# End states' squares folded from 64 to 16 columns a batch by two additions on GpSimd, one product of 64 columns with the means, VectorE sums 64

## Chip, cores and metric

One Trainium2 chip, one of its cores. The metric is device time in microseconds (us), from the first to the last instruction of one execution; lower is better. Engines are named as the profile names them: PE is TensorE (PEld its weight load), DVE is VectorE, ACT is ScalarE, POOL is GpSimd, SP is SyncE.

## What is computed

A state-space block with a residual and a layer norm, then a mixture of experts (8 experts, top 2, capacity 768) with a second residual and layer norm, all float32. The inputs are 8 sequences of 1024 steps of 256 features. The part in question is the recurrence over time, for each sequence, over 512 channels with 16 states each:

```python
def step(h, inp):
    dA_t, dB_t, x_t, C_t, t = inp
    h = h * dA_t + dB_t * x_t[:, :, None]
    nrm = jnp.sqrt(jnp.sum(h * h, axis=(1, 2), keepdims=True))
    fac = jnp.minimum(20.0 / (nrm + 1e-08), 1.0)
    h = jnp.where(t % 10 == 0, h * fac, h)
    y = jnp.einsum('bdn,bn->bd', h, C_t) + D_param * x_t
    return (h, y)
```

At every tenth step the whole state of a sequence (512 x 16 numbers) is scaled by a factor that comes from its norm.

## The kernel before

The recurrence is cut into tiles of T = 20 steps (NB = 52 tiles, index i), each tile into two chunks of 10 steps, and each chunk into two groups of four sequences. A chunk of one group is a batch q (NQ = 208, four batches in a tile; q = 4i + r, and r = 0 to 3 is the batch's place in its tile). Channels lie on the 128 partitions, four blocks a of them. Every engine runs the same loop, `for i in range(-4, NB + 3): for s in range(16)`, where slot s = 4r + u stands for sequence u of batch r. What an engine does in a slot is written by hand, in program order, and semaphores join the engines. There is no scheduler.

In slot u of batch q VectorE writes the products dB*x to PSUM (`mult`, L579), copies in the scaled end states that came out of batch q-2 (`carry`, L596, from tile CAR), and runs the recurrence of sequence u as one scan over 704 columns (`scan`, L610, into H). GpSimd multiplies H by C (L775, into H, one for each u), and TensorE sums these products over the 16 states with the identity (`y_sum`, L816 and L820). Between these stand the pieces of other tiles: projections, convolution, step sizes (ScalarE's L514 and L377 make the decays DA), output projection and norm. `dt_x` on VectorE (L566, twice a tile, in slots 2 and 6, just behind `norm_sum`) multiplies DT and XC, which both lie in SBUF, into PSUM.

The norms go round four engines. After the last scan of batch q-1:

1. ScalarE squares the end states, 4 sequences x 64 columns, into SQ (L398), first in slot u = 0 of batch q.
2. TensorE multiplies SQ by MEAN, a 128 x 128 matrix of 1/256, which sums over the partitions: two products of 4 x 32 = 128 columns (L862), accumulated in `NP`, in slot u = 0 of batch q.
3. VectorE sums `NP` to one number for each sequence (`norm_sum`, L617, tile SN), in slot u = 2, between `mult` and the scan.
4. GpSimd, in slot u = 2 ahead of its product L775: power -0.5 (L755), factor (L757), and end states times factor into CAR (L760).
5. VectorE's `carry` in slot u = 0 of batch q+1 waits for CAR:

```python
if u == 0:
    eng.wait_ge(s_car, q - 1)
eng.tensor_copy(o, CAR[:, u:u + 2]).then_inc(s_ca, 1)
```

GpSimd's other work in a tile: L750 in slot 1, the layer norm's L780, L781, L783 and L786 in slot 3, L793 and L797 in slot 7, L726 in slot 8, L730 in slot 10, L737 and L743 in slot 14.

Of the kernel before, what the change touches and what calls it, by code (L numbers as in the profile page):

```python
# [8 lines left out]
ALU = mybir.AluOpType  # L9
# [9 lines left out]
NQ = 2 * NC  # L19
# [82 lines left out]
def ssm_phase(nc, d, YA, X2d, LGd, Bd, Cd, RB, IOE):  # L102
    ctx = ExitStack()
    with ctx:
        def sb(name, shape, dt=F32):
            return ctx.enter_context(nc.sbuf_tensor(name, shape, dt))

        def sem(name):
            return ctx.enter_context(nc.semaphore(name))
# [11 lines left out]
        MEAN = sb("MEAN", [128, 128])  # L121
# [29 lines left out]
        SQ = sb("SQ", [128, 4, 64])  # L151
# [9 lines left out]
        YB = [ctx.enter_context(nc.psum_tensor(f"YB{i}", [128, 512], F32)) for i in range(2)]  # L161
# [12 lines left out]
        s_bcs, s_ln, s_dth, s_tg, s_z64, s_da, s_x2t, s_hsq = (  # L174
            sem("bcs"), sem("sp"), sem("dth"), sem("tg"), sem("z64"), sem("da"), sem("x2t"), sem("hsq"))

        s_halo, s_sgh, s_dx, s_dxh, s_hc, s_slot = sem("halo"), sem("sgh"), sem("dx"), sem("dxh"), sem("hc"), sem("slot")
        s_min, s_dt, s_xn, s_pow, s_fac, s_car = (
            sem("min"), sem("dt"), sem("xn"), sem("pow"), sem("fac"), sem("car"))
        s_ve, s_sd, s_x2 = sem("ve"), sem("sd"), sem("x2")  # L180
# [2 lines left out]
        s_nrm, s_ys, s_op, s_tr, s_lg = sem("nrm"), sem("ys"), sem("op"), sem("tr"), sem("lg")  # L183
# [22 lines left out]
        def cols(c):  # L206
            return 11 if c < NC - 1 else 1 + (L - 1) % 10


        def rows(c):  # L210
            return min(10, cols(c))
# [12 lines left out]
            return YB[q % 2][:, 0:160]  # L224

        def NP(q):
            return YB[1 - q % 2][:, 256:384]


        def two(j):  # L230
# [2 lines left out]
        def one(j):  # L233
            return 16 * (j // 2 + 1)
# [292 lines left out]
        def vector_program(eng):  # L527
# [85 lines left out]
            def norm_sum(q):  # L613
                eng.wait_ge(s_nrm, q + 1)
                if q >= 2:
                    eng.wait_ge(s_pow, q - 1)
                eng.tensor_reduce(SN[:, q % 2], NP(q).rearrange("p (u a) -> p u a", u=4), AX.X,  # L617
                                  ALU.add).then_inc(s_red, 1)
# [97 lines left out]
        def gpsimd_program(eng):  # L716
            eng.wait_ge(s_pre, PRE_CV)
            for i in range(-4, NB + 3):
                live = ok(i)
                for s in range(16):  # L720
                    r, u = s // 4, s % 4
                    q = 4 * i + r
# [28 lines left out]
                    if u == 2 and 1 <= q <= NQ - 2:  # L751

                        p = q - 1
# [9 lines left out]
                    if i == NB - 2 and s == 0:  # L763

                        k = cols(NC - 1)
                        eng.memset(DA[:, (NC - 1) % 4].rearrange("p b a n t -> p b (a n t)")[:, :, 0:64 * k].rearrange(
                            "p b (a t) -> p b a t", t=k)[:, :, :, 0], 0.0).then_inc(s_slot, 1)
                    if live:
                        k, n = cols(q // 2), rows(q // 2)
                        h = H[:, q % 3, u, 0:64 * k].rearrange("p (a n t) -> p a n t", a=4, n=16)[:, :, :, 0:n]  # L770
                        cb = CB[:, q % 2, :, u, 0:n].unsqueeze(1).to_broadcast([128, 4, 16, n])
                        if u == 0:
                            eng.wait_ge(s_cb[q % 2], one(q))
                        eng.wait_ge(s_scan, 4 * q + u + 1)
                        eng.tensor_tensor(h, h, cb, ALU.mult).then_inc(s_hc, 1)  # L775
# [23 lines left out]
        def tensor_program(eng):  # L799
            def y_sum(q, n0, n1):  # L800
                if not 0 <= q < NQ:
                    return
                k, w = cols(q // 2), rows(q // 2)
                hv = H[:, q % 3, :, 0:64 * k].rearrange("p u (a n t) -> p u a n t", a=4, n=16)
                yv = YP(q).rearrange("p (u a t) -> p u a t", u=4, a=4)[:, :, :, 0:w]
                if n0 == 0:
                    c, g = q // 2, q % 2
                    j, cc = c // 2, c % 2
                    eng.wait_ge(s_dx, j + 1)
                    if j > 0:  # L810
                        eng.wait_ge(s_dxh, j)
                    if q >= 2:
                        eng.wait_ge(s_z, q - 1)
                    if 1 <= q < NQ:
                        eng.wait_ge(s_red, min(q, NQ - 2))
                    eng.matmul(yv, ID[:], DX[:, j % 2, :, 4 * g:4 * g + 4, 10 * cc:10 * cc + w].rearrange(  # L816
                        "p a b t -> p b a t"), start=True, stop=False)
                    eng.wait_ge(s_hc, 4 * (q + 1))
                for n in range(n0, n1):
                    mm = eng.matmul(yv, ID[:], hv[:, :, :, n, 0:w], start=False, stop=n == 15)  # L820
                mm.then_inc(s_ys, 1)
# [28 lines left out]
            for i in range(-4, NB + 3):  # L850
                if i == 0:
                    eng.wait_ge(s_pre, N_PRE)
                for s in range(16):
                    r, u = s // 4, s % 4
                    q = 4 * i + r
                    if u == 0:
                        y_sum(q - 2, 11, 16)
                    if u == 0 and 1 <= q <= NQ - 2:
                        p = q - 1
                        eng.wait_ge(s_hsq, q)  # L860
                        for a in range(2):
                            mm = eng.matmul(NP(p), MEAN[:], SQ[:, :, 32 * a:32 * a + 32], start=a == 0, stop=a == 1)  # L862
                        mm.then_inc(s_nrm, 1)
                    if u == 2:
                        y_sum(q - 1, 0, 6)
                    if u == 3:
# [1 line left out]
                    if s == 0 and ok(i + 3):  # L868
# [3 lines left out]
                        for a in range(2):  # L872
                            mm = eng.matmul(PA[:, 320:480], MEAN[:], TB[:, a].rearrange("p b t -> p (b t)"),
                                            start=a == 0, stop=a == 1)
# [23 lines left out]
                    if s == 7 and ok(i + 2):  # L898
                        j = i + 2
                        dt_proj(j, 0, PZ)  # L900
                        for k in range(4):
                            mm = eng.matmul(PZ[0:64, 320:480], WBC[:, k, :],
                                            XC[:, j % 2, k].rearrange("p b t -> p (b t)"), start=k == 0, stop=k == 3)
                        mm.then_inc(s_dtp, 1)
                    if s == 9 and ok(i - 2):
# [3 lines left out]
                        for g in range(2):  # L909
                            for a in range(2):  # L910
                                mm = eng.transpose(PA[:, 80 * (2 * g + a):80 * (2 * g + a) + 80],
                                                   VV[:, g, 128 * a:128 * a + 128], ID[0:80, 0:80])
                        mm.then_inc(s_tr, 1)
                    if s == 10 and ok(i - 1):
# [4 lines left out]
                        for g in range(2):  # L919
                            for a in range(4):  # L920
                                mm = eng.matmul(PZ[0:80, 256 * g:256 * g + 256], zf[:, a, 80 * g:80 * g + 80],  # L921
                                                WO[:, a, :], start=a == 0, stop=a == 3)
                        mm.then_inc(s_op, 1)
                    if s == 12 and ok(i - 2):
# [3 lines left out]
                        for g in range(2):  # L928
                            for a in range(2):
                                mm = eng.matmul(PA[0:80, 320 + 8 * g:328 + 8 * g], X2T[:, 2 * g + a, :], WR[:, a, :],  # L930
                                                start=a == 0, stop=a == 1)
# [11 lines left out]
        with nc.Block() as block:  # L943
            @block.sync
            def _(eng):
                sync_program(eng)

            @block.scalar
            def _(eng):
                scalar_program(eng)  # L950

            @block.vector
            def _(eng):
                vector_program(eng)

            @block.gpsimd
            def _(eng):
                gpsimd_program(eng)

            @block.tensor  # L960
            def _(eng):
                tensor_program(eng)
# [423 lines left out]
def build(nc, d, out):  # L1386
    YA = nc.dram_tensor("YA", [B * LP, DM], F32, kind="Internal").ap()
    X2d = nc.dram_tensor("X2d", [B * LP, DM], F32, kind="Internal").ap()
    LGd = nc.dram_tensor("LGd", [128, 8 * B, E], F32, kind="Internal").ap()
    Bd = nc.dram_tensor("Bd", [NC, 2, NS, 40], F32, kind="Internal").ap()  # L1390
    Cd = nc.dram_tensor("Cd", [NC, 2, NS, 40], F32, kind="Internal").ap()
    with ExitStack() as ctx:
        RB = ctx.enter_context(nc.sbuf_tensor("RB", [128, 4096], F32))
        IOE = ctx.enter_context(nc.sbuf_tensor("IOE", [128, 8], F32))
        ssm_phase(nc, d, YA, X2d, LGd, Bd, Cd, RB[:], IOE[:])
        moe_phase(nc, d, YA, X2d, LGd, out, RB[:])
# [43 lines left out]
```

## Time and profile before

| what | us |
|---|---|
| median of 3 runs | 2777.07 |
| lowest and highest run | 2772.13, 2777.97 |
| profiled execution, span from first to last instruction | 2772.7 |
| busy in it: PE, DVE, ACT, POOL | 2593.0, 2382.4, 2245.1, 2134.4 |
| granted TensorE clock, mean over the span | 0.975 |

The profile gives the profiled execution's own time as its span; nothing lies around it. The recurrence takes the span from about 100 to 2280 us, and the experts take the rest. A tile of the recurrence takes 42.9 us: GpSimd's L775 of r = 0, slot 0 starts at 1191.37 in one tile and at 1234.26 in the next.

### The profile page before, as it was taken

To read this page: it belongs to the slowest core of one execution; us is meant where nothing else is said; L and a number is where in the kernel's file an instruction comes from. 1 tells how busy PE (TensorE), PEld (TensorE's weight loads), DVE (VectorE), ACT (ScalarE), POOL (GpSimd) and SP (SyncE) were. 2 spreads that over 40 slices of the span, in tenths; PEclk is the share of its full clock that TensorE was granted. 3 is DMA by queue.
4 is the path that set the end of the run, shared out by engine and by line. 5 is a ranking of instruction groups with operands and counts; after the bars stand their busy time and mean duration, and the time that the engine had idled before them with its cause. 6 is when DMAs were issued, how large, how long until landed. Compare 5 with 4: busy or idle time off the path is not lost. (4 is left out here: it accounts for less than half of the span.)

```text
span 2772.7 us, 50775 instructions
## 1 busy us (share of the span) xinstructions
PE 2593.0 (94%) x16812; PEld 2388.8 (86%) x16812; DVE 2382.4 (86%) x3391; ACT 2245.1 (81%) x5074; POOL 2134.4 (77%) x2237
## 2 busy tenths in 40 slices
PE   5899999999999999999999999999999986899992
PEld 4899999999999999999999999999999975677762
DVE  2999999999999999999999999999999997221124
ACT  5999999999999999999999999999999962111113
POOL 0789888898898988989889889898898883434314
PEclk9899999999999999999999999999999987999996
DMA  1222222222222222222222222222222222234227
GB/s 61 70 78 78 79 80 78 78 78 81 77 78 75 80 79 78 78 78 82 78 78 78 81 78 78 76 78 80 78 78 78 75 78 93 48 93 105 61 48 254
DMA packets 145746, 225.65 MB, mean 81 GB/s; under 512 B 37836, under 2 KB 84684, under 8 KB 144332
## 3 DMA queue, kind: packets, MB, share of 16 engines
q1 hardware_dynamic: 123044, 188.95, 22.4%
q0 software_dynamic: 9216, 12.59, 2.6%
q10 hardware_dynamic: 13224, 20.86, 2.2%
q8 instruction: 134, 2.20, 0.3%
q14 instruction: 128, 1.05, 0.1%
HBM read 189.27 MB, written 33.05 MB: 80 GB/s over the span
## 5 line engine op out<-in xcount | busy, mean ns | idle before, releaser
L775 POOL TENSOR_TENSOR H<-H,CB 128x640 f32<-128x640 f32 (+1 forms) x832 | 1216.2, 1476 | 157.1 <-DVE H L610 154.9
L610 DVE TENSOR_TENSOR_SCAN H<-DA,PM 128x704 f32<-128x704 f32 (+1 forms) x832 | 1309.4, 1594 | 0.0
L514 ACT ACTIVATE DA<-DT,SM 128x160 f32<-128x160 f32 (+1 forms) x3328 | 1106.8, 421 | 1.6 <-POOL DT L737 0.3
L820 PE MATMUL YB<-H,ID 128*128 128x160 f32 (+1 forms) x6656 | 1043.9, 309 | 0.2 <-POOL H L775 0.2
L820 PEld LDWEIGHTS YB<-H,ID 128*128 128x128 f32 x6656 | 982.3, 191 | 16.4 <-issue 11.2
L579 DVE TENSOR_TENSOR PM<-PM,BB 128x640 f32<-128x640 f32 (+1 forms) x832 | 673.1, 809 | 0.0
L377 ACT ACTIVATE DA<-DA 128x2560 f32<-128x2560 f32 (+1 forms) x206 | 477.7, 2319 | 1.7
L755 POOL TENSOR_TENSOR FC<-SN,HALF 128x4 f32<-128x4 f32 x206 | 232.8, 1130 | 40.8 <-DVE SN L617 36.8
L826 PE MATMUL PAZ<-XN,RB 128*128 128x160 f32 x1664 | 254.7, 307 | 0.1
L836 PEld LDWEIGHTS PAZ<-XB,CD 128*128 128x128 f32 x1664 | 237.5, 188 | 16.8
L845 PE MATMUL PAZ<-XC,RB 128*128 128x160 f32 x1664 | 244.4, 300 | 3.3 <-DVE XC L647 3.3
L1285 POOL DMA_INDIRECT YA<-YS,IG x48 | 75.1, 1566 | 219.8 <-ACT YS L1116 208.2
L836 PE MATMUL PAZ<-XB,CD 128*128 128x160 f32 x1664 | 243.1, 297 | 0.0
L826 PEld LDWEIGHTS PAZ<-XN,RB 128*128 128x128 f32 x1664 | 237.9, 195 | 0.7 <-ACT CS L467 0.3
L845 PEld LDWEIGHTS PAZ<-XC,RB 128*128 128x128 f32 x1664 | 231.1, 190 | 6.4 <-DVE XC L647 4.0
L921 PE MATMUL PAZ<-WO,Z 128*80 128x256 f32 x832 | 189.1, 380 | 0.0
L862 PE MATMUL YB<-SQ,MEAN 128*128 128x128 f32 x824 | 131.3, 282 | 43.0 <-ACT SQ L398 43.0
L760 POOL TENSOR_TENSOR CAR<-H,FC 128x256 f32<-128x256 f32 x206 | 155.4, 754 | 17.3
L921 PEld LDWEIGHTS PAZ<-WO,Z 128*80 128x80 f32 x832 | 125.3, 151 | 49.4 <-issue 0.7
L1359 PE MATMUL PE<-W,HT 128*128 128x256 f32 x768 | 167.2, 379 | 0.8 <-issue 0.8
L1348 PE MATMUL PE<-XTE,W 128*128 128x384 f32 x512 | 167.3, 488 | 0.0
L1359 PEld LDWEIGHTS PE<-W,HT 128*128 128x128 f32 x768 | 145.3, 190 | 20.8 <-issue 1.3
(157 smaller groups left out, 2779.7 us busy)
## 6 DMA issues: line engine op xcount, KB each, us to landing
BB<-Bd SPq DMA_DIRECT2D x208, 320.0 KB, 3.4
CB<-Cd SPq DMA_DIRECT2D x208, 320.0 KB, 3.2
W<-in_w ACTq DMA_DIRECT2D x16, 1024.0 KB, 7.9
XT<-in_xT SPq DMA_DIRECT2D x52, 160.0 KB, 2.2
XR<-in_xp SPq DMA_DIRECT2D x208, 40.0 KB
X2d<-VV SPq DMA_DIRECT2D x208, 40.0 KB
YA<-VV SPq DMA_DIRECT2D x208, 40.0 KB
HI<-YA SPq DMA_DIRECT2D x6, 1024.0 KB, 9.9
```

Source lines behind the costliest of these rows:

```text
L377: eng.activation(v, v, ACT.Exp, scale=16.0).then_inc(s_da, 1)
L514: eng.activation(DA[:, c0 + k0:c0 + k1, :, a, m, 1:11].rearrange("p c b t -> p b c t"), DT[:, j % 2, a].rearrange("p b (c t) -> p b c t", ...
L579: eng.tensor_tensor(DBX(u)[:, 0:64 * k].rearrange("p (a n t) -> p a n t", a=4, n=16)[:, :, :, 1:k], U(c)[:, :, 4 * g + u, 0:k - 1].unsquee ...
L610: eng.tensor_tensor_scan(H[:, q % 3, u, 0:n], decays(c, g)[:, u], DBX(u)[:, 0:n], 0.0, ALU.mult, ALU.add).then_inc(s_scan, 1)
L755: eng.tensor_tensor(FC[:, p % 2], SN[:, p % 2], HALF[:], ALU.pow).then_inc(s_pow, 1)
L775: eng.tensor_tensor(h, h, cb, ALU.mult).then_inc(s_hc, 1)
L820: mm = eng.matmul(yv, ID[:], hv[:, :, :, n, 0:w], start=False, stop=n == 15)
L826: mm = eng.matmul(p[:, 160 * a:160 * a + 160], WIN[:, k, c0 + 128 * a:c0 + 128 * a + 128], XN[:, j % 2, k], start=k == 0, stop=k == 1)
L836: mm = eng.matmul(p[:, 160 * a:160 * a + 160].rearrange("p (b t) -> p b t", b=8), CD[:, k, 2 * m + a], XB[:, 2 * m + a, :, k:k + 20], star ...
L845: mm = eng.matmul(p[:, 160 * a:160 * a + 160], WDT[:, k, c:c + 128], XC[:, j % 2, k].rearrange("p b t -> p (b t)"), start=k == 0, stop=k == 3)
L921: mm = eng.matmul(PZ[0:80, 256 * g:256 * g + 256], zf[:, a, 80 * g:80 * g + 80], WO[:, a, :], start=a == 0, stop=a == 3)
L1359: t = eng.matmul(bank(n)[:, 256 * h:256 * h + 256], HT[:, m, 128 * (2 * c + h):128 * (2 * c + h) + 128], W2[:, e % 2, m, :], start=m == 0, ...
```

## The change

The squares are folded on GpSimd before they go to TensorE. At the start of slot u = 0 of every batch, ahead of its product L775, GpSimd waits for SQ, adds columns 32 to 63 of each sequence to columns 0 to 31, waits for that, and adds columns 16 to 31 to 0 to 15. TensorE then does one product of 4 x 16 = 64 columns where it did two of 128, and does it in slot u = 1 in place of u = 0. VectorE sums 64 numbers to 4 where it summed 128 to 4. The result is the same up to the order of additions.

```diff
@@
+        s_half, s_fold = sem("half"), sem("fold")
@@
         def NP(q):
-            return YB[1 - q % 2][:, 256:384]
+            return YB[1 - q % 2][:, 256:320]
@@ gpsimd_program
+                    if u == 0 and 1 <= q <= NQ - 2:
+
+                        eng.wait_ge(s_hsq, q)
+                        eng.tensor_tensor(SQ[:, :, 0:32], SQ[:, :, 0:32], SQ[:, :, 32:64], ALU.add).then_inc(s_half, 1)
+                        eng.wait_ge(s_half, q)
+                        eng.tensor_tensor(SQ[:, :, 0:16], SQ[:, :, 0:16], SQ[:, :, 16:32], ALU.add).then_inc(s_fold, 1)
                     if live:
@@ tensor_program
-                    if u == 0 and 1 <= q <= NQ - 2:
+                    if u == 1 and 1 <= q <= NQ - 2:
                         p = q - 1
-                        eng.wait_ge(s_hsq, q)
-                        for a in range(2):
-                            mm = eng.matmul(NP(p), MEAN[:], SQ[:, :, 32 * a:32 * a + 32], start=a == 0, stop=a == 1)
-                        mm.then_inc(s_nrm, 1)
+                        eng.wait_ge(s_fold, p + 1)
+                        eng.matmul(NP(p), MEAN[:], SQ[:, :, 0:16], start=True, stop=True).then_inc(s_nrm, 1)
```

On GpSimd this is the stretch from slot 7 to slot 10 of a tile (r = 1 to r = 2), before the change, with the semaphores that each instruction waits for:

```order
L793 TENSOR_TENSOR DX<-XC,SM 128x32x20 [waits xc,ys]
L797 COPY DX<-DX 128x32
L726 COPY XB<-XB 128x32x3 [waits cv]
L775 TENSOR_TENSOR H<-H,CB 128x64x10 [waits scan,cb0]
L775 TENSOR_TENSOR H<-H,CB 128x64x10 [waits scan]
L730 TENSOR_SCALAR TA<-TA 128x640 [waits ex]
L755 TENSOR_TENSOR FC<-SN,HALF 128x4 [waits red]
L757 TENSOR_SCALAR FC<-FC 128x4 [waits pow]
L760 TENSOR_TENSOR CAR<-H,FC 128x256 [waits ca,fac]
```

And with the change (its lines are numbered anew: L782 is L775, L756 is L755, and so on):

```order
L800 TENSOR_TENSOR DX<-XC,SM 128x32x20 [waits xc,ys]
L804 COPY DX<-DX 128x32
L727 COPY XB<-XB 128x32x3 [waits cv]
L772 TENSOR_TENSOR SQ<-SQ 128x4x32 [waits hsq]
L774 TENSOR_TENSOR SQ<-SQ 128x4x16 [waits half]
L782 TENSOR_TENSOR H<-H,CB 128x64x10 [waits scan,cb0]
L782 TENSOR_TENSOR H<-H,CB 128x64x10 [waits scan]
L731 TENSOR_SCALAR TA<-TA 128x640 [waits ex]
L756 TENSOR_TENSOR FC<-SN,HALF 128x4 [waits red]
L758 TENSOR_SCALAR FC<-FC 128x4 [waits pow]
L761 TENSOR_TENSOR CAR<-H,FC 128x256 [waits ca,fac]
```

The two additions stand ahead of four long instructions and of the three that make CAR. The same pair stands in this place in the other three batches of a tile.

On TensorE this is the stretch around the product with the means in the tile's batch r = 1, before the change:

```order
L820 MATMUL YB1<-H,ID 128x160 x5
L862 MATMUL YB1<-SQ,MEAN 128x128 x2
L816 MATMUL YB0<-DX,ID 128x160
L820 MATMUL YB0<-H,ID 128x160 x6
L845 MATMUL PAZ<-XC,RB 128x160 x8
```

And with the change:

```order
L827 MATMUL YB1<-H,ID 128x160 x5
L868 MATMUL YB1<-SQ,MEAN 128x64
L823 MATMUL YB0<-DX,ID 128x160
L827 MATMUL YB0<-H,ID 128x160 x6
L852 MATMUL PAZ<-XC,RB 128x160 x8
```

In this batch the product keeps its neighbours, since slot 4 and slot 5 hold nothing else. In r = 0 it moves behind the eight projections of slot 0, in r = 3 behind the four products of L930 and the first four of the gate's projections.

## Rows read from the trace of the kernel before

**Rows 1.** The page's head: the span, and each engine's busy time, share and instructions.

```profile
span 2772.7 us, 50775 instructions
PE 2593.0 (94%) x16812; PEld 2388.8 (86%) x16812; DVE 2382.4 (86%) x3391; ACT 2245.1 (81%) x5074; POOL 2134.4 (77%) x2237
```

**Rows 2.** Busy time by stretch: stretch, length, engines in order, clock, DMA share, GB/s.

```profile
core 0: us, PE busy (x) PEld busy (x) DVE busy (x) ACT busy (x) POOL busy (x), PEclk, DMA share, GB/s
1000.00:1400.00 400.00, 393.46 (x2724) 373.77 (x2724) 400.00 (x544) 384.12 (x859) 354.45 (x373) 1.00 0.27 78
```

**Rows 3.** Waits in 200 to 2200 us: waiter, releaser, total, times, longest.

```profile
POOL H L775 <- DVE H L610: 132.5, 138, 2.0
PE YB L862 <- ACT SQ L398: 34.2, 47, 0.7
POOL FC L755 <- DVE SN L617: 26.7, 94, 0.4
```

**Rows 4.** Timeline of POOL over one tile: start, duration (x2: both together), [idle before].

```profile
1194.88 1.22 POOL L755 TENSOR_TENSOR FC<-SN,HALF 128x4 f32<-128x4 f32 x1 [0.34 <-DVE SN L617]
...
1202.66 2.92 POOL L775 TENSOR_TENSOR H<-H,CB 128x640 f32<-128x640 f32 x2
...
1205.80 1.25 POOL L755 TENSOR_TENSOR FC<-SN,HALF 128x4 f32<-128x4 f32 x1 [0.22 <-DVE SN L617]
...
1212.67 3.00 POOL L775 TENSOR_TENSOR H<-H,CB 128x640 f32<-128x640 f32 x2
...
1216.56 1.03 POOL L755 TENSOR_TENSOR FC<-SN,HALF 128x4 f32<-128x4 f32 x1
...
1218.00 0.75 POOL L760 TENSOR_TENSOR CAR<-H,FC 128x256 f32<-128x256 f32 x1
1218.70 2.91 POOL L775 TENSOR_TENSOR H<-H,CB 128x640 f32<-128x640 f32 x2
1222.29 1.47 POOL L775 TENSOR_TENSOR H<-H,CB 128x640 f32<-128x640 f32 x1 [0.68 <-DVE H L610]
...
1229.32 2.92 POOL L775 TENSOR_TENSOR H<-H,CB 128x640 f32<-128x640 f32 x2
1234.26 1.48 POOL L775 TENSOR_TENSOR H<-H,CB 128x640 f32<-128x640 f32 x1 [2.01 <-DVE H L610]
```

**Rows 5.** Timeline of DVE in the same tile.

```profile
1205.44 0.28 DVE L617 TENSOR_REDUCE SN<-YB 128x4 f32<-128x128 f32 x1
1205.66 0.50 DVE L566 TENSOR_TENSOR PM<-DT,XC 128x320 f32<-128x320 f32 x1
...
1219.62 0.28 DVE L596 COPY PM<-CAR 128x128 f32<-128x128 f32 x1
...
1230.78 0.16 DVE L714 COPY LGS<-PAZ 80x16 f32<-80x16 f32 x1
```

**Rows 6.** Groups of POOL by shape, whole span: count, busy us, mean ns, idle before.

```profile
L760 POOL TENSOR_TENSOR CAR<-H,FC 128x256 f32<-128x256 f32 x206 | 155.4, 754 | 17.3
L743 POOL TENSOR_TENSOR XN<-XT,RST 128x320 f32<-128x320 f32 x52 | 45.0, 865 | 20.9 <-ACT RST L493 14.0 <-PE PAZ L826 3.6
L775 POOL TENSOR_TENSOR H<-H,CB 128x256 f32<-128x256 f32 x8 | 5.7, 734 | 3.0 <-DVE H L610 2.9
L1298 POOL TENSOR_TENSOR NM<-NM,SD 128x8 f32<-128x8 f32 x8 | 1.6, 202 | 0.6
```

**Rows 7.** Timeline of POOL and DVE in one later batch; DVE L566 by itself (ns min/median/max).

```profile
2232.02 2.91 POOL L775 TENSOR_TENSOR H<-H,CB 128x640 f32<-128x640 f32 x2
2234.89 1.25 POOL L755 TENSOR_TENSOR FC<-SN,HALF 128x4 f32<-128x4 f32 x1
...
2234.31 0.97 DVE L566 TENSOR_TENSOR PM<-DT,XC 128x320 f32<-128x320 f32 x1
...
L566 DVE TENSOR_TENSOR PM<-DT,XC x104: 480/494/974, 54.0 to 2266.7; 128x320 f32<-128x320 f32 x104
```

**Rows 8.** Timeline of PE at the product with the means, r = 1 and r = 0.

```profile
1202.22 0.61 PE L862 MATMUL YB<-SQ,MEAN 128*128 128x128 f32 x4
1202.66 0.45 PE L816 MATMUL YB<-DX,ID 128*128 128x160 f32 x2
...
1231.52 0.71 PE L862 MATMUL YB<-SQ,MEAN 128*128 128x128 f32 x4 [0.72 <-ACT SQ L398]
```

## The prediction

> **What bounds the kernel now.** I read the head of the page first: PE is busiest over the whole span [rows 1], but the experts' stage has other limits, so the shares of the span don't decide. The stretches come next. In 400 us of the recurrence DVE is busy for 400.00, PE for 393.46, ACT for 384.12 and POOL for 354.45 [rows 2]. So VectorE sets the pace of the recurrence. The waits agree: POOL waits for DVE's scans and sums, TensorE waits for the squares once a tile, and DVE is nowhere among the waiters [rows 3]. PE runs so close behind that its load has to be watched, but taking work off it gives nothing by itself.
>
> POOL has 354.45 of 400 us filled, which leaves 4.9 us a tile of 42.9, and part of that is the hand-over between dependent instructions. What matters is where it lies. In one tile [rows 4] it waits 0.34 before the power of r = 0, 0.22 before that of r = 1, 0.68 before the first product of r = 3, and 2.01 before the first product of r = 0. Between the power of r = 1 (1205.80) and 1222.29 it is packed. The first two waits occur 94 times in 2000 us and sum to 26.7, which is two a tile in 47 tiles and 0.57 a tile, as in this tile [rows 3]. CAR of r = 2 is finished at 1218.75, and DVE's copy that needs it starts at 1219.62 [rows 4, 5]: 0.87 us of slack.
>
> **The change, part by part.**
>
> *VectorE's sum.* 128 columns take 0.28, and an instruction of 16 columns from PSUM takes 0.16 [rows 5]. That is 1.07 ns a column, so 64 fewer save 0.07 us. On the full engine this is gain: four a tile, 0.28 us a tile. Without any wait, 52 tiles would give 14.5 us.
>
> *TensorE.* The two products are four instructions in 0.61 us with the tail, and the next group starts 0.44 after the first [rows 8]. Half as many, of half the columns, take at most half, so about 0.25 a batch is saved, 1 us a tile; the wait of 0.72 before the squares of r = 0 goes too. PE isn't the pace, so this counts as nothing in the sum. It pays for the new wait: in r = 1 the product was ready to start at 1202.22, and the fold will be done only at about 1203.4, since POOL starts it at 1202.6. PE loses about 1.1 us there and regains it by r = 0 of the next tile. What DVE needs from the product in that batch is its sum at 1205.44, so 1.5 us of cover are left.
>
> *The fold itself, f.* The trace has no such addition. Two-input instructions of POOL take 0.202 us for 8 columns, 0.734 and 0.754 for 256, and 0.865 for 320 [rows 6]. From 8 to 320 that is 2.12 ns a column. So 128 columns come to 0.457 and 64 to 0.321. The second waits for the first: POOL's instructions that wait for another's result start 0.08 after its end (1205.44 + 0.28 = 1205.72 to 1205.80) [rows 4, 5]. Packed ones overlap by 0.03. I take **f = 0.84 us**. The bounds: below, two of the 8-column kind and the hand-over, 0.45; above, two of the 256-column kind, 1.5. Rows of 256 columns and over lie close on one line with the row of 8, so I expect 0.70 to 1.0.
>
> *Where it goes.* I carry lateness against the tile before along POOL. DVE's first sum of the tile is 0.07 early, so POOL arrives at the fold of r = 1 0.07 early. The two products that started at 1202.66 and took 2.92 now end at 1202.66 - 0.07 + f + 2.92 = 1206.35.
>
> DVE's L566 wants to start at 1205.66 - 0.14 = 1205.52, in the middle of the second product. This is the first place where it matters. In the whole trace L566 takes 494 ns in the median and once 974: at 2234.31, when POOL's second L775 was still running until 2234.93. It ended at 2235.28, 0.35 after POOL's instruction [rows 7]. It is the only two-input instruction of the loop with both inputs in SBUF on DVE. So with the fold L566 ends at 1206.35 + 0.35 = 1206.70 where it ended at 1206.16: **DVE is 0.54 late, in every tile.** The power behind it starts 0.5 late, and takes 1.25 as in that row.
>
> One delayed row is thin evidence. The Trainium skill (SBUF — State Buffer, Who interferes with whom) says that VectorE with two SBUF inputs contends with a GpSimd instruction that reads SBUF, and that whoever starts first keeps the port for its whole instruction. By this the row is the rule and the delay recurs; the power's 1.25 beside L566 and 1.03 elsewhere [rows 4] fits it. Were the row a chance, the sum would be that of the second rival below.
>
> POOL is then 0.51 late through the products of r = 1 and L793, L797, L726. The second fold, before 1212.67, makes it 0.51 + 0.84 = 1.35. CAR of r = 2 is done at 1218.75 + 1.35 = 1220.10, and with the hand-over of 0.08 DVE can copy it at 1220.18. DVE itself would be there at 1219.62 + 0.54 - 0.07 = 1220.09. So the copy starts 0.56 late, and CAR now decides, just. What is queued behind the copy on DVE is the product and the four scans of r = 3, and everything else of the loop.
>
> *Recovery.* The fold of r = 3 starts at 1218.70 + 2.91 + 1.35, about 1222.96, and ends at 1223.8: the wait of 0.68 is gone, and POOL is 1.5 late at the first product. In r = 0 it has 2.01 of idle: the products end at 1229.32 + 2.92 + about 1.25 = 1233.5, the fold at 1234.3, and the product waits anyway for DVE's scan, now at 1234.26 + 0.5. So each tile starts anew, and nothing piles up.
>
> *Sum.* DVE is 0.56 late at the copy, gains 0.07 at the sum of r = 3, and ends **0.49 us a tile late**. As a formula: with the port wait f - 0.44, with CAR 2f - 1.19, whichever is more. The layer norm's work that packs POOL in slot 3 runs from tile 2 on, so 50 tiles have both places: 50 x 0.49 = 24.5 us. The profiled span becomes 2772.7 + 24.5 = 2797.2. Its span is 4.4 below the median of the runs, so the median goes from 2777.07 to 2801.6; I say **2801**.
>
> **Rivals.** A change under 0.2% (5.5 us) counts as none, which is about what a measurement of this kernel can tell from no change.
>
> *The fold is hidden and VectorE's shorter sums show: faster.* For: DVE is full, so 0.28 us a tile is real. The place is the second product of r = 1. This rival needs it to be out of L566's way and CAR in time. From the formulas it decides at f = 0.44 with the port wait; without that wait (next rival) there is no loss below f = 0.70 and the full gain below 0.56. f would have to be like two instructions of 8 columns, against rows of 256 that take over 0.7. Full gain: 2777 - 14 = 2763. Chance 8%.
>
> *L566 does not wait in each tile.* Then the power of r = 1 starts past it and takes 1.03, not 1.25. POOL is 0.29 late at the power's end and 0.29 + 0.84 = 1.13 at CAR of r = 2: 1219.96 with the hand-over, 0.34 late, less 0.07 is 0.27 a tile, 13 us: 2790. Against: the row of 974 ns. Chance 15%.
>
> *Near zero.* The same with f of 0.70: 2 x 0.14 less, so about nothing, 2777. Chance 8%.
>
> *It does not recover in r = 0, or TensorE becomes the pace.* POOL's idle in the listed waits is 3.25 a tile, and four folds take 3.36. If f is 1.0, the formula gives 0.81 a tile, and the last fold ends at about 1235.2, past DVE's scan, so that the sum of r = 0 begins to be late too: 0.9 to 1.2 a tile, 2822 to 2837. TensorE's 1.1 us at r = 1 could add to it if its 6.5 idle us in 400 do not cover them: they do in the account above, as 1 us a tile is saved. Chance 10%.
>
> The forecast, f between 0.70 and 1.0 with the port wait, has the other 59%: 0.26 to 0.81 a tile, 2790 to 2818.
>
> **Numbers.** The range of 2783 to 2820 takes in the forecast's own and most of the second rival; it leaves out the gain, no change, and the piling up. Slower by over 0.2%: 59 + 15 + 10 = 84%. No change is the near-zero case, 8%, and faster is the first rival, 8%.
>
> **What the trace of the changed kernel would show.** The additions: two a batch, near 0.46 and 0.32 us, 206 each. The sum L617: 0.21 us. L566: half of its 104 at about 1.0 us, half at 0.49. CAR's copy in r = 3: idle of DVE just before it, or none if the port wait alone decides. POOL: no wait before its first product of r = 3, about 0.5 to 1 left in r = 0. A new wait of TensorE for the fold, about 1 us, once a tile. The tile: 43.4 us in place of 42.9. I would be wrong if the additions were much shorter than their columns say, or if L566 ran beside POOL's product at its usual length.

## The result: 0.8% slower, and the profile after

| | before | changed |
|---|---|---|
| median of 5 runs, us | 2776.85 | 2797.32 |
| lowest and highest | 2771.82, 2777.97 | 2796.19, 2798.49 |
| span of the profiled execution | 2772.7 | 2795.3 |
| one tile of the recurrence | 42.89 | 43.32 |

The ratio is 1.0081 (95% interval 1.0068 to 1.0093), which is 20.5 us slower by the medians and 22.6 by the spans. "One tile" is the time from GpSimd's copy of SG (L750, L751 after) in one tile to that in the next, the median over 49 or 50 tiles of a trace. It differs by 0.03 us or less between nearly all tiles, so it tells apart what the runs' scatter of 3 to 6 us does not. In the traces every tile from the second on loses the 0.43: the copies of SG from the second to the last are 21.5 us further apart, the first tile is 2.1 us shorter than before, and 0.4 come ahead of the first copy. The other 2.7 of the 22.6 lie behind the last copy, where the change does nothing; that part takes 508 to 513 us over the traces of this study. So the loss that the change makes is in the recurrence, in every tile, and the rest is scatter or not explained.

The page's head of the changed kernel, which answers to [rows 1]:

```profile
span 2795.3 us, 50363 instructions
PE 2555.7 (91%) x16400; PEld 2343.1 (84%) x16400; DVE 2402.9 (86%) x3391; ACT 2256.9 (81%) x5074; POOL 2278.6 (82%) x2649
```

The stretch that answers to [rows 2]:

```profile
1000.00:1400.00 400.00, 383.16 (x2629) 362.44 (x2628) 399.90 (x535) 383.11 (x861) 377.06 (x444) 1.00 0.26 77
```

POOL went from 354.45 to 377.06 busy us of 400, and PE from 393.46 to 383.16. DVE is still "busy" for 399.90, and that is the trap of this profile: it does the same work at a slower pace, because one of its instructions has become longer. The groups of DVE and POOL show which. First DVE between 200 and 2200 us, by shape:

```profile
L567 DVE TENSOR_TENSOR PM<-DT,XC 128x320 f32<-128x320 f32 x92 | 71.9, 782 | 0.5
...
L618 DVE TENSOR_REDUCE SN<-YB 128x4 f32<-128x64 f32 x185 | 37.7, 204 | 0.0
```

And POOL over the whole span:

```profile
L772 POOL TENSOR_TENSOR SQ<-SQ 128x128 f32<-128x128 f32 x206 | 94.3, 458 | 2.9 <-ACT SQ L399 2.9
...
L774 POOL TENSOR_TENSOR SQ<-SQ 128x64 f32<-128x64 f32 x206 | 66.2, 321 | 16.2
```

L567 (L566 before) had a median of 494 ns [rows 7] and now has a mean of 782: it alternates between 0.49 us in r = 0 and 1.07 in r = 1. The waits between 200 and 2200 us, against [rows 3]:

```profile
PE PAZ L878 <- ACT TB L409: 50.0, 46, 1.1
...
PE YB L868 <- POOL SQ L774: 36.5, 47, 0.9
...
POOL H L782 <- DVE H L611: 25.6, 47, 0.9
POOL FC L756 <- DVE SN L618: 12.6, 46, 0.3
```

POOL's wait for scans fell from 132.5 to 25.6, and its wait for the sum stands once in a tile now, where it stood twice. DVE has no such wait (one of 0.3 us in all): while L567 is held up it counts as busy. One tile on POOL (answers to [rows 4]):

```profile
1200.36 1.47 POOL L782 TENSOR_TENSOR H<-H,CB 128x640 f32<-128x640 f32 x1 [0.52 <-DVE H L611]
...
1211.56 0.45 POOL L772 TENSOR_TENSOR SQ<-SQ 128x128 f32<-128x128 f32 x1
1212.09 0.32 POOL L774 TENSOR_TENSOR SQ<-SQ 128x64 f32<-128x64 f32 x1
1212.37 2.92 POOL L782 TENSOR_TENSOR H<-H,CB 128x640 f32<-128x640 f32 x2
1215.24 1.30 POOL L756 TENSOR_TENSOR FC<-SN,HALF 128x4 f32<-128x4 f32 x1
...
1228.25 0.75 POOL L761 TENSOR_TENSOR CAR<-H,FC 128x256 f32<-128x256 f32 x1
```

And on DVE (answers to [rows 5]):

```profile
1203.51 0.21 DVE L618 TENSOR_REDUCE SN<-YB 128x4 f32<-128x64 f32 x1
1203.64 0.49 DVE L567 TENSOR_TENSOR PM<-DT,XC 128x320 f32<-128x320 f32 x1
...
1214.36 0.22 DVE L618 TENSOR_REDUCE SN<-YB 128x4 f32<-128x64 f32 x1
1214.59 1.07 DVE L567 TENSOR_TENSOR PM<-DT,XC 128x320 f32<-128x320 f32 x1
...
1228.33 0.80 DVE L580 TENSOR_TENSOR PM<-PM,BB 128x640 f32<-128x640 f32 x1
1229.10 0.29 DVE L597 COPY PM<-CAR 128x128 f32<-128x128 f32 x1
```

The reader is to lay these two fences over each other. POOL's second product of r = 1 ends at 1212.37 + 2.92 = 1215.29. DVE's L567 stands in its queue from 1214.59, and ends at 1215.66, 0.37 after POOL's product. It is the same in each of 40 tiles: L567 starts 2.2 behind the start of GpSimd's two products and ends 0.35 to 0.37 behind their end. In r = 0 POOL's products are over in time and the same instruction takes 0.49. Later, CAR is done at 1229.00 and the copy starts at 1229.10; packed, it would start 0.71 to 0.72 behind the product of 1228.33, at 1229.05. That is 0.05 of wait, in every tile.

### The profile page after: what moved, and what is told of

Its sections match the earlier page's. It is cut to its first block and busy times, and to the rows that moved or that the text cites. A ratio compares the mean times of both kernels' runs of the same rounds, so it can differ in the third digit from the quotient of the medians.

```text
span 2795.3 us, 50363 instructions
## 1 busy us (share of the span) xinstructions
PE 2555.7 (91%) x16400; PEld 2343.1 (84%) x16400; DVE 2402.9 (86%) x3391; ACT 2256.9 (81%) x5074; POOL 2278.6 (82%) x2649
## 3 DMA queue, kind: packets, MB, share of 16 engines
q14 instruction: 131, 1.07, 0.1%
## 5 line engine op out<-in xcount | busy, mean ns | idle before, releaser
L782 POOL TENSOR_TENSOR H<-H,CB 128x640 f32<-128x640 f32 (+1 forms) x832 | 1211.6, 1475 | 38.2 <-DVE H L611 37.8
L833 PE MATMUL PAZ<-XN,RB 128*128 128x160 f32 x1664 | 264.4, 308 | 0.4 <-DVE VV L698 0.2
L756 POOL TENSOR_TENSOR FC<-SN,HALF 128x4 f32<-128x4 f32 x206 | 234.8, 1140 | 21.5 <-DVE SN L618 17.5
L1121 ACT ACTIVATE YS<-YS,GT 128x256 f32<-128x256 f32 x48 | 21.8, 500 | 172.9 <-DVE YS L1230 172.9
```

Of the source, the lines that this page charges most:

```text
L833: mm = eng.matmul(p[:, 160 * a:160 * a + 160], WIN[:, k, c0 + 128 * a:c0 + 128 * a + 128], XN[:, j % 2, k], start=k == 0, stop=k == 1)
```

## Experiments

Times are compared with runs of the kernel before on the same chip, whose medians were 2775.5, 2773.8 and 2775.6 us in the three groups (e1 to e4, e5 to e8, e9 to e12).

### Which fold costs: e1, e2, e6, e11

The fold is done only in the batches r of a set, the others keep the old two products and the sum of 128 (the edit in part; TensorE's side and the size of the sum follow the same set):

```diff
+        FOLD = [0, 1, 3]        # e1; [0, 2, 3] in e2, [0, 3] in e6, [1] in e11
-                    if u == 0 and 1 <= q <= NQ - 2:
+                    if u == 0 and 1 <= q <= NQ - 2 and q % 4 in FOLD:
                         eng.wait_ge(s_hsq, q)
```

**e1, no fold in r = 2.**

> The changed kernel without the fold in the tile's batch r = 2 (there the old two products of 128 columns and the sum of 128). Theory (port wait): L567 (L572 here) of r = 1 still finds GpSimd's second product running, since the fold of r = 1 stands: it takes about 1.07 us in that batch, VectorE is 0.51 late behind it, and gets 0.07 back in r = 3: 0.44 us a tile, 22 us, 2799, the same as the changed kernel within 3 us, with no wait for CAR. Rival (only the late CAR of r = 2 costs): GpSimd is in time for r = 2's CAR, three shorter sums show, 0.21 a tile: 2767.

Measured: 2796.85 (2795.24 to 2797.78), ratio 1.0078 (1.0061 to 1.0095), tile 43.34. L567's counterpart takes about 1.08 in r = 1. It is the changed kernel's time with a quarter of GpSimd's new work gone. So the late CAR of r = 2 is not what costs, but for a few hundredths of a microsecond (e10).

**e2, no fold in r = 1.**

> The changed kernel without the fold in r = 1, with it in r = 0, 2 and 3. Theory: GpSimd is in time at L567 of r = 1, which takes 0.49 in all batches; the fold of r = 2 uses up the 0.87 of slack of CAR (late by at most 0.09), three shorter sums gain 0.21: 0.12 to 0.21 us a tile faster than before, 2767 to 2771. Rival (GpSimd's load decides, wherever the fold stands): three quarters of the loss stay, 2792.

Measured: 2771.22 (2770.04 to 2771.70), ratio 0.9986 (0.9976 to 0.9996), tile 42.74. The product of DT and XC takes 0.49 and 0.50 in all batches. Three folds of four cost next to nothing, and the kernel is about 0.15% faster than before, less than the 0.2% that the prediction counts as a change. That refutes the rival by which GpSimd's load decides, wherever the fold stands.

**e6, folds in r = 0 and r = 3.**

> The changed kernel with the fold only in r = 0 and r = 3, the two batches in which GpSimd waited before the change (2.01 and 0.68 us); r = 1 and r = 2 have the old products and sums. Theory: both folds fit the waits, two shorter sums gain 0.14 us a tile: tile 42.75, 2769 to 2770. Rival (three folds are better because more sums are shorter): 2.8 us slower than the kernel without the fold in r = 1 alone; or, if CAR of r = 2 was late there, the same or faster than it.

Measured: 2766.70 (2765.47 to 2768.20), ratio 0.9974 (0.9963 to 0.9985), tile 42.75. The tile agrees with the 42.75 expected. It is also that of e2 within 0.01 us: the third shorter sum of e2 gains about 0.06, and CAR of r = 2 takes 0.05 back. The 4.5 us between the medians of e2 and e6 are for the most part not in the tiles: of the 3.1 us between their traces 1.1 are there and 1.9 behind the last tile. Their groups differ by 1.8 us in the kernel before, and the rest stays unexplained.

**e11, the fold in r = 1 alone.**

> The fold in r = 1 alone, everything else as before the change. Theory: this one fold holds the whole loss and none of the gain, since VectorE's product behind the sum of r = 1 waits for another instruction anyway: VectorE 0.58 late a tile, tile 43.47, 2806. Rival (the loss needs all four folds): a quarter of it or nothing, 2772 to 2782.

Measured: 2805.17 (2803.32 to 2805.65), ratio 1.0110 (1.0094 to 1.0125), tile 43.48. One fold of four costs 0.59 us a tile, more than all four together. This is the plainest evidence in the set: its place makes the loss, and the other three only soften it.

### Is it the port: e3

VectorE's product in slot 6 takes PSUM numbers in the place of DT (the factor is left out for every other chunk):

```diff
-                eng.tensor_tensor(U(c), DT[:, j % 2, :, :, t], XC[:, j % 2, :, :, t], ALU.mult).then_inc(s_u, 1)
+                dt = DT[:, j % 2, :, :, t]
+                if c % 2 == 0 and c > 0:
+                    eng.wait_ge(s_m1, 8 * c - 9)
+                    dt = DBX(0)[:, 0:320].rearrange("p (a b t) -> p a b t", a=4, b=8)
+                eng.tensor_tensor(U(c), dt, XC[:, j % 2, :, :, t], ALU.mult).then_inc(s_u, 1)
```

> The changed kernel, but VectorE's product of DT and XC in slot 6 (the one behind the sum of r = 1) takes PSUM numbers in DT's place, so it leaves that factor out for every other chunk: one input in SBUF, all sizes, folds and waits else as changed. Theory (port wait): it takes about 0.5 us in place of 1.07 although GpSimd's product still runs; the power behind it takes 1.03; what is left is CAR of r = 2, late by 0.28 less 0.07: 0.21 us a tile, 2788. Rival (the instruction is long for another reason than its SBUF inputs): 1.07 and 2797 as in the changed kernel.

Measured: 2784.26 (2783.62 to 2785.96), ratio 1.0035 (1.0022 to 1.0048), tile 43.08. The two kinds of the product by themselves (ns min/median/max), between 200 and 2200 us DVE's copy of CAR with its idle time, and the place in one tile, POOL and then DVE:

```profile
L571 DVE TENSOR_TENSOR PM<-DT,XC x53: 480/486/646, 53.8 to 2273.0; 128x320 f32<-128x320 f32 x53
L571 DVE TENSOR_TENSOR PM<-PM,XC x51: 498/500/500, 89.5 to 2240.8; 128x320 f32<-128x320 f32 x51
```

```profile
L601 DVE COPY PM<-CAR 128x128 f32<-128x128 f32 x372 | 105.0, 282 | 10.2 <-POOL CAR L765 10.1
```

```profile
1205.52 2.93 POOL L786 TENSOR_TENSOR H<-H,CB 128x640 f32<-128x640 f32 x2
...
1207.81 0.50 DVE L571 TENSOR_TENSOR PM<-PM,XC 128x320 f32<-128x320 f32 x1
```

With one input from PSUM the instruction never exceeds 500 ns, at the same place (2.29 us behind the start of GpSimd's two products, 2.22 in the changed kernel), with the same size. It ends at 1208.31, and GpSimd's products at 1208.45. What kept it waiting is therefore its second SBUF input. The remaining 0.19 us a tile (43.08 against 42.89) is what the working of the prediction's second rival gives for the late CAR without the port wait: 2f - 1.41, which is 0.27 with its f of 0.84 and 0.21 with the measured 0.81. The row shows CAR's wait as idle time, 10.1 us in 45 tiles, 0.22 a tile.

### Gain and cost apart: e4, e7

**e4** leaves the additions out (three quarters of the squares are missing from the norms) and keeps the rest (first GpSimd's side, then TensorE's):

```diff
-                        eng.wait_ge(s_hsq, q)
-                        eng.tensor_tensor(SQ[:, :, 0:32], SQ[:, :, 0:32], SQ[:, :, 32:64], ALU.add).then_inc(s_half, 1)
-                        eng.wait_ge(s_half, q)
-                        eng.tensor_tensor(SQ[:, :, 0:16], SQ[:, :, 0:16], SQ[:, :, 16:32], ALU.add).then_inc(s_fold, 1)
+                        pass
...
-                        eng.wait_ge(s_fold, p + 1)
+                        eng.wait_ge(s_hsq, p + 1)
```

> The changed kernel without the two additions: the product takes the first 16 columns of the squares, so three quarters of them are left out of the norms. All other sizes and places as changed. Theory: only the shorter sum of VectorE is left, 0.27 us a tile: tile 42.62 us, 2763. Rival (VectorE's sum gives nothing, or the product's new place costs): 2777 or more.

Measured: 2765.34 (2763.57 to 2767.33), ratio 0.9967 (0.9954 to 0.9979), tile 42.69. The gain is real, but it is 0.20 us a tile and not 0.27. TensorE's load falls in this run too, by about 0.27 us a batch; a shorter sum with TensorE's load as before was not run.

**e7** keeps the additions and their waits, but gives products and sum their old sizes (some squares count more than once):

```diff
-            return YB[1 - q % 2][:, 256:320]
+            return YB[1 - q % 2][:, 256:384]
...
-                        eng.matmul(NP(p), MEAN[:], SQ[:, :, 0:16], start=True, stop=True).then_inc(s_nrm, 1)
+                        for a in range(2):
+                            mm = eng.matmul(NP(p), MEAN[:], SQ[:, :, 32 * a:32 * a + 32], start=a == 0, stop=a == 1)
+                        mm.then_inc(s_nrm, 1)
```

> The changed kernel with the additions and their waits, but products and VectorE's sum at their old sizes (two of 128 columns over the squares after the additions, so the norms count some squares more than once). Theory: the cost alone, without the gain: VectorE 0.58 us late in each tile behind the port wait, nothing gained: tile 43.47, 2777 + 29 = 2806; a little more if TensorE's larger load (about 0.25 us a batch) with the wait in r = 1 makes it late. Rival (the additions cost what the changed kernel lost, the sums gain nothing): 2797.

Measured: 2806.65 (2805.96 to 2807.72), ratio 1.0117 (1.0100 to 1.0134), tile 43.48. The cost alone is 0.59 us a tile, as in e11, and as expected.

### Does TensorE's new wait cost: e5

The additions go to columns 32 to 63 of SQ, and the product takes columns 0 to 15 without waiting for them (three quarters of the squares are left out). So that ScalarE doesn't overwrite squares that are still being added, it waits for the additions before it squares again:

```diff
+                            eng.wait_ge(s_fold, q - 1)
...
-                        eng.tensor_tensor(SQ[:, :, 0:32], SQ[:, :, 0:32], SQ[:, :, 32:64], ALU.add).then_inc(s_half, 1)
+                        eng.tensor_tensor(SQ[:, :, 32:64], SQ[:, :, 0:32], SQ[:, :, 32:64], ALU.add).then_inc(s_half, 1)
                         eng.wait_ge(s_half, q)
-                        eng.tensor_tensor(SQ[:, :, 0:16], SQ[:, :, 0:16], SQ[:, :, 16:32], ALU.add).then_inc(s_fold, 1)
+                        eng.tensor_tensor(SQ[:, :, 32:48], SQ[:, :, 32:48], SQ[:, :, 48:64], ALU.add).then_inc(s_fold, 1)
...
-                        eng.wait_ge(s_fold, p + 1)
+                        eng.wait_ge(s_hsq, p + 1)
```

> The changed kernel with the additions written to columns 32 to 63 of the squares, and a product that takes columns 0 to 15 and waits for the squares alone: three quarters of the squares are left out of the norms. GpSimd does the same two additions at the same places; TensorE no longer waits for them (0.78 us a tile in the changed kernel). Theory: TensorE's wait is covered, the time stays at 2797 within 3 us, tile 43.3. Rival (that wait costs part of the loss): up to 0.4 us a tile less, 2777 to 2790.

Measured: 2797.78 (2796.21 to 2801.22), ratio 1.0084 (1.0067 to 1.0100), tile 43.32. TensorE's wait for the fold costs nothing. In its place TensorE waits elsewhere in the tile, for DVE's VV (38.6 us in 46 tiles).

### The fold on TensorE: e8

This run starts from the kernel before; GpSimd has nothing new, and VectorE sums 64 numbers.

```diff
-            return YB[1 - q % 2][:, 256:384]
+            return YB[1 - q % 2][:, 256:320]
...
-                        for a in range(2):
-                            mm = eng.matmul(NP(p), MEAN[:], SQ[:, :, 32 * a:32 * a + 32], start=a == 0, stop=a == 1)
+                        for a in range(4):
+                            mm = eng.matmul(NP(p), MEAN[:], SQ[:, :, 16 * a:16 * a + 16], start=a == 0, stop=a == 3)
```

> The kernel before with the fold done by TensorE's accumulation: four products of 64 columns into the same 64, in place of two of 128; VectorE sums 64; GpSimd has nothing new. If a product of 64 columns takes 0.08 us an instruction (the next group starts 0.16 after the first of two in the changed kernel): TensorE 0.1 to 0.2 us a batch more, inside its 0.7 us of idle a tile, and VectorE's gain shows: 2763. If it takes as long as one of 128 columns (0.11 to 0.14): 0.5 us a batch more, TensorE becomes the pace: 1 to 1.5 us a tile slower, 2830 to 2850.

Measured: 2852.67 (2851.46 to 2853.35), ratio 1.0283 (1.0266 to 1.0301), tile 44.55. That is the second case, and a little beyond its 2830 to 2850. The stretch of 400 us, the waits between 200 and 2200 us, and two places on TensorE:

```profile
1000.00:1400.00 400.00, 393.47 (x2768) 375.57 (x2767) 385.49 (x522) 371.11 (x827) 341.61 (x360) 1.00 0.26 76
```

```profile
DVE SN L617 <- PE YB L862: 40.8, 45, 0.9
...
DVE H L610 <- ACT DA L377: 31.4, 45, 1.0
...
PE YB L862 <- ACT SQ L398: 32.6, 45, 0.7
```

```profile
1217.97 1.00 PE L862 MATMUL YB<-SQ,MEAN 128*128 128x64 f32 x8
1218.81 0.69 PE L930 MATMUL PAZ<-WR,X2T 128*80 128x8 f32 x8
...
1227.39 1.10 PE L862 MATMUL YB<-SQ,MEAN 128*128 128x64 f32 x8 [0.72 <-ACT SQ L398]
```

The four products take 0.84 us to the start of the next group, where the two of 128 columns took 0.44 [rows 8]. Four batches of 0.40 more are 1.6 us a tile, and the tile lost 1.66. DVE now waits, for TensorE's product and for decays that ScalarE makes late: TensorE has become the pace. So "TensorE runs close behind" was true, and the shorter sum cannot be bought there. The idle 0.7 us a tile that TensorE had is still there, as the same wait for the squares of r = 0 (34.2 us in 47 tiles before [rows 3], 32.6 in 45 now): it was no room for more work. Through which instructions the added time comes round to VectorE was not followed up.

### Repairs: e9, e10, e12

All three move GpSimd's minimum of slot 10 (L730, 0.72 us) behind CAR of the same slot.

**e9**, with folds in r = 0, 2 and 3:

> Fold in r = 0, 2 and 3, and GpSimd's minimum of slot 10 (L730, 0.72 us) moved behind CAR of r = 2. Theory: nothing waits; three shorter sums gain all that the run without additions gained: tile 42.69, 2763 to 2766. Rival (the minimum is needed at once by ScalarE): 42.75 or more.

Measured: 2765.71 (2764.72 to 2769.41), ratio 0.9967 (0.9955 to 0.9979), tile 42.69. This is the tile of e4, now with the additions done: nothing waits.

**e10**, with all four folds:

> The changed kernel with all four folds, and the minimum of slot 10 moved behind CAR of r = 2, so that CAR comes 0.8 us earlier. Theory: the port wait in r = 1 alone sets the loss, CAR's lateness added only 0.05: tile 43.27, 2794 to 2795. Rival (CAR of r = 2 is what is late): tile 42.7 to 42.9, 2765 to 2777.

Measured: 2794.46 (2794.21 to 2794.66), ratio 1.0070 (1.0055 to 1.0086), tile 43.27. CAR 0.8 us earlier gives 0.05 us, as expected; the port wait holds the rest.

**e12** also puts VectorE's product of slot 6 behind that slot's scan:

```diff
-                    if s == 6 and ok(i + 1):
-                        dt_x(2 * i + 2)
                     if live:
                         scan(q, u)
+                    if s == 6 and ok(i + 1):
+                        dt_x(2 * i + 2)
```

> All four folds, the minimum moved behind CAR as in e10, and VectorE's product of DT and XC in slot 6 put behind that slot's scan, where GpSimd is in its power (1.03 us) and no longer in the long product. Theory: the port wait shrinks from 0.58 to 0.1 or 0.3, tile 42.75 to 42.95, 2767 to 2779. Rival (the product waits as long wherever it stands): 43.2 or more.

Measured: 2762.53 (2760.80 to 2764.27), ratio 0.9957 (0.9942 to 0.9972), tile 42.59. The place in its trace, first POOL:

```profile
1236.12 2.94 POOL L782 TENSOR_TENSOR H<-H,CB 128x640 f32<-128x640 f32 x2
1239.00 1.05 POOL L752 TENSOR_TENSOR FC<-SN,HALF 128x4 f32<-128x4 f32 x1
```

And DVE:

```profile
1238.06 0.26 DVE L618 TENSOR_REDUCE SN<-YB 128x4 f32<-128x64 f32 x1
1238.19 1.66 DVE L611 TENSOR_TENSOR_SCAN H<-DA,PM 128x704 f32<-128x704 f32 x1
1239.72 0.52 DVE L567 TENSOR_TENSOR PM<-DT,XC 128x320 f32<-128x320 f32 x1
```

The scan starts at 1238.19, while POOL's product still runs to 1239.06, and is not held up. The product of DT and XC starts after POOL's product, in the midst of the power. It waits not at all, though 0.1 to 0.3 was expected: every VectorE instruction is recorded 0.03 to 0.05 longer in this trace (the scan 1.65 for 1.60) and starts as close behind the last as ever, so its 0.52 is its usual length. All four sums show their gain. This is the fastest kernel of the study, 13 us (0.43%) faster than before, with the change's own diff kept whole. What the two moves would give without any fold was not run.

## Why the prediction was right

**The pace.** VectorE was the pace before and after. e4 and e6 show that a shorter sum there is a gain, e5 that a wait of TensorE isn't a loss, and e8 that more load on TensorE is. By e8 TensorE was closer behind than I thought: its idle time covered none of the 1.6 us that were added. The change gave it less to do, so this did not touch the forecast.

**The shorter sum, 0.28 us a tile: mis-sized.** It is 0.20 (e4). The instruction did become 0.07 shorter in each batch, and the next starts 0.13 after it where it was 0.20. But in r = 1 L567 still starts 0.23 behind the sum (1214.36 to 1214.59), as it did before (0.22, [rows 5]). It waits for the last product of that chunk in any case, since it overwrites a buffer which that product reads. I counted four gains where only three can show. In e12 the scan takes that place, and the fourth shows: 42.59 against 42.69, its 0.07 and about 0.03 that the wait for the buffer had cost. In the changed kernel the error cost the forecast nothing, since there the end of GpSimd's product decides when L567 ends, whenever it would have started.

**The fold, f = 0.84.** The additions take 0.458 and 0.321, against 0.457 and 0.321 from the line through POOL's rows. From the first addition's start to the product's it is 0.81 (1211.56 to 1212.37). The hand-over between them is the 0.08 that I took. My own terms, 0.457 + 0.08 + 0.321 - 0.03 for the overlap, make 0.83, not the 0.84 I wrote, and the measured pieces are 0.02 less again. The formula doubles these 0.03.

**The port wait, 0.54 in each tile.** Right. From the sum of r = 0 to the end of L567 in r = 1 VectorE took 11.63 us before (1194.53 to 1206.16) and takes 12.15 now (1203.51 to 1215.66): 0.52 late, with the 0.07 gained in r = 0 taken off; the instruction alone is 0.58 longer. The sum of r = 0 in the trace of before:

```profile
1194.53 0.27 DVE L617 TENSOR_REDUCE SN<-YB 128x4 f32<-128x128 f32 x1
```

The wait is shown from four sides: it vanishes when the fold of r = 1 goes (e2), when one input comes from PSUM (e3) and when the instruction stands elsewhere (e12), and it stays when everything else goes (e11). The one row of 974 ns in the old trace was the rule. The Trainium skill (SBUF — State Buffer, Who interferes with whom) states that a VectorE instruction with two SBUF inputs contends with a GpSimd instruction that reads SBUF, and e3 agrees: with one input from PSUM the 1.07 us became 0.50. That whoever starts first keeps the port for its whole instruction agrees with GpSimd's products, and not with its power (e12, see the last section).

**CAR of r = 2.** The copy was to start 0.56 late, at 1220.18, 0.09 after VectorE could be there (1220.09). Right: it is 0.50 late against the sum of r = 0 (25.59 us where it was 25.09), and 0.05 after VectorE could be there (e10). With the measured f the same terms give 0.50 and 0.06. Without the port wait this path alone costs 0.19 a tile (e3).

**Recovery in r = 0.** Right: POOL still has 0.52 of idle there (I said 0.5 to 1), and tiles do not pile up. TensorE's wait at r = 1 was 0.78, not 1.1, and was covered (e5).

**The sum.** 2f - 1.19 with the measured f of 0.81 is 0.43 us a tile, and the traces give 43.32 - 42.89 = 0.43. Times 50 this is 21.5 us, against 24.5 predicted, 22.6 by the spans and 20.5 by the medians. That the sum over the tiles is so near both is partly luck: the first tile took 2.1 us off it in the traces, and the time ahead of and behind the tiles gave 3.1 back.

Of the rivals, the hidden fold fell because the additions took what their columns say. "L567 does not wait" was made real by e3: 2784.3, 0.19 a tile, where I had 2790 and 0.27 with the larger f. The third needed no port wait and a fold of 0.70, and had neither. The fourth fell with POOL's idle time in r = 0, though TensorE had less to spare than it supposed (e8).

## What to carry to other kernels

Before giving GpSimd more work, list the instructions of VectorE that read both inputs from SBUF, and see what GpSimd runs when each of them comes up: the cost sits at that meeting, not in the added busy time. In this kernel three of the four folds cost nothing or 0.05 us, and the fourth cost 0.59 us, with the same two instructions. A VectorE that is "100% busy" can still be waiting; compare an instruction's longest with its median (974 and 494 ns in the trace of before), since this wait showed there and not as idle time. Then move the instruction that collides, rather than take back the change.

## What the hardware did that was not expected

- VectorE's product with two SBUF inputs waited for GpSimd's long two-input products to their end (ending 0.35 to 0.37 us after them), but ran beside GpSimd's power of four columns without delay: 0.52 us in e12, started 0.72 us into the power and ended 0.19 after it, with the power at 1.05 instead of 1.03. That differs from the rule cited in the prediction, by which the power, having started first, would have held the port to its end. Started the other way round, the power beside the product takes 1.21 to 1.30. Which part of the power uses the port was not tried.
- In float32 a product of 64 columns was hardly cheaper than one of 128 when several stood in a row. To the start of the next group four instructions of 128 columns take 0.44 us [rows 8] and eight of 64 take 0.84 (e8), 0.11 and 0.105 each. The two of the changed kernel's single product take 0.17, 0.08 each, as here in r = 2:

```profile
1223.47 0.33 PE L868 MATMUL YB<-SQ,MEAN 128*128 128x64 f32 x2
1223.64 0.45 PE L916 MATMUL PAZ<-ID,VV 80*128 80x80 f32 x4
```

So halving the columns of a product and doubling their number nearly doubled its cost; narrower and wider products were not tried.
